# Macaron block, one core: a new order of the work ahead of the first exponential

## What is computed

```python
x = x + 0.5 * ffn(layernorm(x))          # layernorm inside ffn too; ternary weight, bias
x = x + attention(layernorm(x))          # q,k,v,o 512x512, rope, 64-token blocks, causal by block
x = x + 0.5 * ffn(layernorm(x))
# attention, per head (32 channels):
scores = einsum('bhqd,bhkd->bhqk', rope(q), rope(k)) * D**-0.5
ctx = einsum('bhqk,bhkd->bhqd', softmax(where(block_mask, scores, -inf)), v)
```

## Time and profile before

| | us |
|---|---|
| median of 3 runs (636.68 to 638.52) | 636.81 |
| the profiled execution | 636.18 |
| its span, from first to last instruction | 634.4 |
| TensorE busy (matmul) | 554.8 (87%) |
| VectorE busy | 409.6 (65%) |
| ScalarE busy | 310.5 (49%) |
| GpSimd busy | 238.9 (38%) |

### The profile page before, as it was taken

The page is one execution under the profiler, slowest core; times in us unless marked ns, Lnnn a source line. Parts: engine busy times, 40 slices in busy tenths (PEclk is TensorE's granted clock), DMA queues, the critical chain, the costliest instruction groups (busy, mean ns, idle before and its releaser), DMA issues.

```text
span 634.4 us, 10072 instructions
## 1 busy us (share of the span) xinstructions
PE 554.8 (87%) x3586; PEld 235.4 (37%) x3586; DVE 409.6 (65%) x782; ACT 310.5 (49%) x629; POOL 238.9 (38%) x200
## 2 busy tenths in 40 slices
PE   0785799679878999999999999999999898998866
PEld 0542545334323333333333333333344233343432
DVE  5999656626878668667677677677667822522462
ACT  0831622122215756756756666666656456661320
POOL 4001454443656547547556556556500100100100
PEclk9897899899979999999999999999999999999897
DMA  9930022363222125323123126323410021101011
GB/s 313 355 118 25 2 74 92 116 154 123 76 75 76 52 77 175 118 76 109 52 77 107 58 76 208 97 81 119 133 36 2 2 80 71 50 6 55 8 67 66
DMA packets 43602, 57.95 MB, mean 91 GB/s; under 512 B 3527, under 2 KB 34375, under 8 KB 42529
## 3 DMA queue, kind: packets, MB, share of 16 engines
q1 hardware_dynamic: 42972, 57.21, 27.5%
q10 hardware_dynamic: 580, 0.11, 0.1%
HBM read 32.01 MB, written 25.17 MB: 90 GB/s over the span
## 4 chain that ended last, share of the span: by engine, by line
PE 69%; DVE 23%; issue 3%; ACT 2%; DMA 1%; POOL 1%; SPq 0%; ACTq 0%; DVEq 0%; POOLq 0%
PE bank L956 11%; PE bank L1045 10%; PE bank L920 9%; PE bank L939 9%; PE bank L1055 8%; PE bank L874 7%; PE bank L884 6%; PE bank L993 5%; DVE rmax L815 5%; DVE stats L661 3%; DVE mparts L828 3%; DVE rmax L825 2%; PE bank L864 2%; DVE big L676 2%; DVE kst L676 1%
## 5 line engine op out<-in xcount | busy, mean ns | idle before, releaser
L815 DVE TENSOR_REDUCE rmax<-bank 128x1 f32<-128x512 f32 (+3 forms) x384 | 198.8, 551 | 107.7 <-PE bank L939 105.2
L609 ACT ACTIVATE big<-bank 128x512 f32<-128x512 f32 (+3 forms) x384 | 181.6, 492 | 141.9 <-PE bank L920 138.8
L939 PE MATMUL bank<-kst,qst 104*128 104x512 f16 (+3 forms) x384 | 126.2, 331 | 23.0 <-DVE rmax L815 16.4
L920 PE MATMUL bank<-qst,kst 106*128 106x512 f16 (+3 forms) x384 | 125.8, 329 | 3.1 <-ACT big L609 2.8
L502 POOL TENSOR_TENSOR rot<-t,sin_s 64x512 f32<-64x512 f32 x64 | 82.1, 1282 | 92.5 <-ACT t L602 89.8
L1045 PE MATMUL bank<-big,ones 128*32 128x512 f32 (+3 forms) x768 | 81.8, 498 | 0.0
L1055 PE MATMUL bank<-big,rows 128*32 128x512 f32 (+3 forms) x768 | 79.5, 486 | 0.0
L920 PEld LDWEIGHTS bank<-qst,kst 106*128 106x128 f16 x384 | 36.9, 96 | 89.9 <-issue 39.3
L511 POOL TENSOR_TENSOR rhl<-t,rhl 128x512 f16<-128x512 f32 x32 | 37.5, 1172 | 70.0 <-ACT rhl L623 70.0
L939 PEld LDWEIGHTS bank<-kst,qst 104*128 104x128 f16 x384 | 37.9, 99 | 64.2 <-DVE rmax L815 22.8
L956 PE MATMUL bank<-xh,wh 128*128 128x512 f16 x128 | 50.3, 393 | 6.3 <-DVE xl L697 5.9
(11 more groups left out here) (106 smaller groups left out, 688.6 us busy)
## 6 DMA issues: line engine op xcount, KB each, us to landing
spread<-rhl SPq DMA_DIRECT2D x32, 256.0 KB, 2.2
qst<-spread SPq DMA_DIRECT2D x16, 384.0 KB, 3.8
kst<-spread SPq DMA_DIRECT2D x16, 384.0 KB, 3.9
x<-rows SPq DMA_DIRECT2D x4, 1024.0 KB, 4.6
spread<-rhl SPq DMA_DIRECT2D x32, 128.0 KB, 2.1
rows<-in_L_attn_x_dram SPq DMA_DIRECT2D x3, 1024.0 KB, 15.4
xh<-ch SPq DMA_DIRECT2D x4, 512.0 KB, 5.5
xl<-cl SPq DMA_DIRECT2D x4, 512.0 KB, 6.7
```

Of the source, the lines that this page charges most:

```text
L609: nc.scalar.activation(probs[:, st % P_PLACES, h, 0:n], pb[u % 2][:, 0:n], ACT.Exp, scale=EXP_SCALE).then_inc(s_eb, 1)
L815: nc.vector.tensor_reduce(rmax[:, at:at + 1], a_bank(u)[:, 0:n], AX.X, ALU.max, negate=True).then_inc(s_max, 1)
L920: nc.tensor.matmul(pb[u % 2][:, 0:n], kst[0:ROWS_B, g % SETS, h, j * P:(j + 1) * P], qst[0:ROWS_B, g % SETS, h, q0:q0 + n], start=True, st ...
L939: nc.tensor.matmul(a_bank(u)[:, 0:n], qst[0:ROWS_A, g % SETS, h, i * P:(i + 1) * P], kst[0:ROWS_A, g % SETS, h, half * HALF:half * HALF + ...
```

## The change

The diff, cut where lines repeat what is told here. SECOND, the steps of the second batch and of its second block move, v_unit starts a tile every seven steps in the first batch and leaves steps 56 to 67 free; the second batch's transposes and products all use banks 3 and 4 in turn; loads and splits of weights come in the order q, v, k, o; waits are on high parts first and on low parts where they are read; the small operations of the maxima come after the reduction of the next step.

```diff
-        y1_bank = [bank[0:8], [bank[n % 5] for n in range(8)]]
+        y1_bank = [bank[0:8], bank[3:5] * 4]
         f1_bank = [bank[0:4] * 2, bank[3:5] * 4]
-        x_bank = [bank[4:8] + bank[0:4], [bank[n % 3] for n in range(8)]]
+        x_bank = [[bank[i] for i in (4, 0, 1, 2, 3, 4, 0, 1)], bank[3:5] * 4]
...
+        W_ORDER = (0, 2, 1, 3)
+        def weight_parts(i):
+            return W_ORDER.index(i) + 1
...
-            n, i = divmod(k - lag, 6)
-            if 0 <= n < BATCH * TILES:
-                return n // TILES, n % TILES, i
+            for n in range(BATCH * TILES):
+                i = k - lag - (7 * n if n < TILES else 68 + 6 * (n - TILES))
+                if 0 <= i < 6:
+                    return n // TILES, n % TILES, i
...
-        SECOND = 5
-        Y1_STEP = [7 + n for n in range(8)]
-        F1_STEP = [17 + 3 * r for r in range(8)]
-        S2_STEP = [30, 42]
-        N2_STEP = [34, 46]
-        X_STEP = [36 + n for n in range(4)] + [48 + n for n in range(4)]
+        SECOND = 18
+        N1_STEP = [24, 46]
+        Y1_STEP = [28, 30, 32, 34, 51, 53, 55, 57]
+        F1_STEP = [38, 41, 44, 47, 67, 70, 73, 76]
+        S2_STEP = [51, 80]
+        N2_STEP = [58, 85]
+        X_STEP = [61, 62, 63, 64, 88, 89, 90, 91]
...
@@ SyncE @@
             load_w(0, w_q)
+            load_w(2, w_v)
             load_w(1, w_k)
...
-            load_w(2, w_v)
...
-            sp.wait_ge(s_wl, 2)
-            mask_rows(0, 1)
             residual_out(0, 0)
             residual_out(0, 1)
+            sp.wait_ge(s_wl, weight_parts(1))
+            mask_rows(0, 1)
...
-                    if k == STEPS + 16 + 6 * bl:
+                    if k == X_STEP[4 * bl + 3] + 7:
                         columns_out(bl)
...
-                if k == STEPS + 10:
+                if k == X_STEP[3] + 4:
                     sp.wait_ge(s_wl, 4)
+                    sp.wait_ge(s_xtr[1], 4)
+                if k == X_STEP[7] + 4:
                     sp.wait_ge(s_xtr[1], 8)
                     mask_rows(1, SETS)
...
@@ GpSimd @@
-            rstd_of(1, 0, 5)
-            rstd_of(1, 1, 6)
-            roots = 6
+            roots = 4
...
+                    if k == N1_STEP[bl] - 2:
+                        rstd_of(1, bl, 5 + bl)
+                        roots = 5 + bl
...
@@ VectorE, ahead of the loop @@
-            for n in range(4):
-                weight_low(1, n)
+            ffn_update(4, f1_bank[0], blocks[0], s_ffn1[0], s_up1[0])
+            ffn_update(5, f1_bank[0], blocks[0], s_ffn1[0], s_up1[0])
             dve.wait_ge(s_ytr1[0], 4)
             normalize(0, 0, 3, blocks[0][0], y1[0][0], s_y2[0])
-            for r in range(4, 8):
-                ffn_update(r, f1_bank[0], blocks[0], s_ffn1[0], s_up1[0])
-            dve.wait_ge(s_up1[0], 8)
-            statistics(0, 1, 4, *ONCE, blocks[0][1])
+            ffn_update(6, f1_bank[0], blocks[0], s_ffn1[0], s_up1[0])
+            ffn_update(7, f1_bank[0], blocks[0], s_ffn1[0], s_up1[0])
             for n in range(4):
                 x_low(0, n)
             for n in range(4):
                 weight_low(2, n)
+            dve.wait_ge(s_up1[0], 8)
+            statistics(0, 1, 4, *ONCE, blocks[0][1])
+            for n in range(4):
+                weight_low(1, n)
...
@@ VectorE, in the loop @@
-                if k == 2:
-                    normalize(1, 0, 5, blocks[1][0], y1[1][0], s_y1[1])
-                    dve.wait_ge(s_x[1][1], 16)
-                    statistics(1, 1, 6, *TWICE, blocks[1][1])
...
+                if k == N1_STEP[0]:
+                    normalize(1, 0, 5, blocks[1][0], y1[1][0], s_y1[1])
+                if 36 <= k < 40:
+                    weight_low(3, k - 36)
+                if k == 40:
+                    dve.wait_ge(s_x[1][1], 16)
+                    statistics(1, 1, 6, *TWICE, blocks[1][1])
+                if k == N1_STEP[1]:
                     normalize(1, 1, 6, blocks[1][1], y1[1][1], s_y1[1])
-                if 16 <= k < 20:
-                    weight_low(3, k - 16)
...
-                if e := max_head(k, 0):
+                if e := max_head(k, 1):
...
@@ TensorE @@
+                    if u == 0:
+                        pe.wait_ge(s_xl[1], 8)
...
                         if g < 2:
                             pe.wait_ge(s_rows[g], 32)
-                            pe.wait_ge(s_xl[1], 8)
...
-                            pe.wait_ge(s_xl[0], 4 * (m // 2) + 4)
-                            pe.wait_ge(s_wl, 2)
+                            pe.wait_ge(s_xh[0], 4 * (m // 2) + 4)
...
+                    if g == 0 and CC in SLOTS[i]:
+                        pe.wait_ge(s_xl[0], 4 * (m // 2) + 4)
+                    if g == 0 and 2 * CC in SLOTS[i]:
+                        pe.wait_ge(s_wl, weight_parts(m % 2))
...
-                        pe.wait_ge(s_xl[b], 4 * (r // 4) + 4)
-                        pe.wait_ge(s_wl, 3)
+                        pe.wait_ge(s_xh[b], 4 * (r // 4) + 4)
...
+                    if i == 2:
+                        pe.wait_ge(s_xl[b], 4 * (r // 4) + 4)
+                    if i == 4:
+                        pe.wait_ge(s_wl, weight_parts(2))
...
                         pe.wait_ge(s_y1[1], 4 * (n // 4) + 4)
-                        pe.wait_ge(s_xl[0], 8)
-                        if n >= 5:
-                            pe.wait_ge(s_f1[1], n - 4)
+                        if n < 2:
+                            pe.wait_ge(s_xl[0], 8)
+                        elif n in (4, 5):
+                            pe.wait_ge(s_up1[1], n - 1)
+                        else:
+                            pe.wait_ge(s_f1[1], n - 1)
...
-                        if n >= 3:
-                            pe.wait_ge(s_xl[1], n - 2)
+                        if n < 2:
+                            pe.wait_ge(s_f1[1], n + 7)
+                        elif n in (4, 5):
+                            pe.wait_ge(s_up1[1], n + 3)
                         else:
-                            pe.wait_ge(s_f1[1], n + 6)
+                            pe.wait_ge(s_xl[1], n - 1)
...
-                        pe.wait_ge(s_f1[1], 5)
-                        if r >= 2:
+                        if r < 2:
+                            pe.wait_ge(s_f1[1], r + 3)
+                        elif r in (4, 5):
+                            pe.wait_ge(s_xl[1], r - 1)
+                        else:
                             pe.wait_ge(s_up1[1], r - 1)
```

More of the change, by code:

```diff
@@ L574, in _ @@
                 columns1(0, n)
[L575 to L578, removed]
+            for i in W_ORDER:
+                weight_high(i)
             for n in range(4):
@@ L724, in weight_low @@
             def weight_low(i, cc):
-                dve.wait_ge(s_wh, i + 1)
+                dve.wait_ge(s_wh, weight_parts(i))
                 last = nc.vector.scalar_tensor_tensor(wl[:, i, cc, :], stage[i][:, cc, :], W_SCALE, wh[:, i, cc, :],
@@ L903, in _ @@
             for cc in range(CC):
+                if cc:
+                    pe.wait_ge(s_up1[0], 4 + cc)
                 transposed(x_bank[0][cc], y1[0][0], cc, s_xtr[0])
```

## The result

The changed kernel takes 612.93 us (median of 4, 610.56 to 614.11) against 637.66 in the same comparison; the ratio is 0.9606 with a 95% interval of 0.9569 to 0.9642. Twice more, in other comparisons, it was 0.9631 (0.9613 to 0.9649) and 0.9651 (0.9631 to 0.9671). The profiled execution took 612.61, its span 610.8.

A forecast was written before the change was run, and what follows sets the result against it. TensorE was taken to bound the exponential stretch (372.9 of 389.0 us busy), while the two stretches before lost 37 us. Span 634.4 - 21 - 4.6 = 608.8, 610.5 us after adjustment and rounding; range 602 to 624, the forecast's own 604 to 617.

The forecast's parts named there:

- Part 1: Start of the step loop: step 0 waits for high parts only and comes at 45.0 us, 5.8 us earlier.
- Part 2: Steps 0 to 58: 46.7 us of TensorE work plus 7.6 of waits, so step 59 is reached at 99.3 us.
- Part 3: Steps 59 to 117: 55.1 us of work plus waits at three places; step 118 at 169 us, 21 us earlier.
- Place (a): Steps 61 to 64, waiting for a normalization and the fourth projection's way: idle some 7 us, then 2 us for half clock.
- Place (b): Steps 80 to 91: VectorE has 16.4 us of work against TensorE's 11.4, costing 5 us.
- Place (c): Last transposes before step 118 each wait for a fresh low part, 1 us; first value product behind them, 0.5.
- Part 4: Maxima's small operations one step later: about 0.3 us saved at each of 16 fourth-score waits, 4.6 us; bounds 0 and 13.
- slow clock through the stretch: Rival: frequent waits keep the granted clock at 1.2 GHz from step 60 on; time 653 us, chance 0.03.
- gain paid back in the exponentials: Rival: something starting no earlier (GpSimd, transfers) sets the exponential stretch and takes the gain back; 636 us, chance 0.02.
- Half the gain: Rival: VectorE's long operations hold the score banks more often, two more wait and half-clock pairs; 623 us, or 618; chance 0.17.

The follow-up runs named there:

- e7: The changed kernel unchanged, run again as the measure for three others: 615.17 us, ratio 0.9651 to the kernel before.
- e5: The changed kernel with step 0 waiting also for the low parts and the value weights' low part: 617.70 us, ratio 0.9696.
- e10: Changed kernel, copy before scale and shift, rotary of four tiles held behind normalizations, one normalization before the weight split, two tiles' high parts two steps later: 610.09 us.
- e4: The changed kernel with one GpSimd wait: rotary of step 81's tile starts only after the second batch's last normalization: 610.11 us, ratio 0.9581.
- e1: The changed kernel with the small operations of the maxima back in their old place: 617.37 us, ratio 0.9680.
- e8: The kernel before with only the small operations of the maxima one step later: 629.19 us, ratio 0.9869.
- e9: The changed kernel with ScalarE's projection copy ahead of the scale and shift, and two tiles' rotary held behind normalizations: 610.54 us, ratio 0.9577.
- e11: The changed kernel with the small operations in their old place for the first group's four heads only: 612.00 us, ratio 0.9594.

## Why the prediction was right

610.5 us were forecast, 612.9 measured; 26.3 us of gain, 24.7 measured. The total is nearer than its terms, and that is luck: the start of the loop came 3.0 us late and steps 59 to 117 took 3.1 more, while the exponential stretch gave 2.3 more than its term and the tail behind it 1.6 that no term had (0.2 in e7). Two slips in the prediction's sum are small: 16 x 0.3 is 4.8 and not 4.6, and 611.2 was rounded to 610.5. The steps, by their own numbers:

- **Part 1, start of the loop**: 45.0 forecast, 47.97 measured, 45.2 in e7. The chain was right to 0.2 us; the rest is the granted clock of the products ahead, which the earlier trace rows show at full rate, so the forecast took it as given. In nine traces of kernels that start the products alike the distance from the first product to step 0 was 18.3 us where all products ran at full clock (e7), 19.7 to 20.1 in seven whose first products took 1.91 us, and 21.2 in the changed kernel's first profile, where this lasted longest. e5 shows that a later start costs time at the end.
- **Part 2, steps 0 to 58**: 54.3 forecast, 54.2 measured. The work was counted; the waits came to the same sum from other places. Step 18 waited 2.98 (forecast 2.1), its normalization took 4.74 (nearly 5). Step 28 did not wait (2.7 forecast). A copy and a feed-forward product took 0.87 and 0.97 us. The idle times come to 5.1 us where 7.6 were forecast, and a half clock 3.4 us long behind step 18, which the forecast left out, cost 1.7. That the sum met to 0.1 us is in part luck. The sentence that this would be 5 us less if the normalizations took 1.91 is not borne out: only one of the two waits was there to be gained, and in e10, where all normalizations took 1.9, holding the rotary back brought waits of its own and the stretch took 54.6.
- **Part 3, steps 59 to 117**: 69.7 forecast, 72.8 and 73.5 measured. Place (a): idle 4.9 us instead of 7, half clock 5.5 us long instead of 4; its wait is ScalarE's queue at step 60 and the normalization, not the transfer. Place (b): 1.42, 0.57, 3.10 and 0.24 make 5.3 us (5 forecast). What was left out is the half clock behind it, 4.7 us at 0.64, which e4 removes along with the wait. Place (c): 0.3 instead of 1.5; 0.8 at step 111 was not foreseen. In all TensorE was idle 11.3 us (13.5 forecast), and the granted clock of 0.93 over 72.8 us cost up to 5.1 (2 forecast). So the term that was too small is the clock's, in (b) above all; e7 has 10.7 us of idle time and up to 6.8 of clock.
- **Part 4, small operations**: 4.6 forecast. The exponential stretch shows 6.5 to 7.6 (e1), 5.8 (e8). Per group of four heads it is 46.86 us in e1 and 45.73 in the changed kernel, for two waits: 0.5 to 0.6 each and not 0.3. The mechanism (fourth score at once, fifth waits) is as described, 0.34 and 0.17 us at the fifth instead of 0.86 and 0.64 at the fourth. In the medians only 2.3 to 3.1 us of it are seen (e1). The forecast took the small operations' 1.86 us as their own length. It is mostly GpSimd's, as e4 shows for one head: they took 1.9 to 2.3 us in the 27 heads of the kernel before with rotary work beside them, and 0.57 in the four heads behind with none (timeline of VectorE, the last of the three operations, beside the rotary and alone):

```profile
250.45 1.11 DVE L828 SCALAR_TENSOR_TENSOR mparts<-rmax,mparts 128x8 f16<-128x8 f32 x1
...
461.91 0.17 DVE L828 SCALAR_TENSOR_TENSOR mparts<-rmax,mparts 128x8 f16<-128x8 f32 x1
```

  No run keeps the rotary off them all along the exponential stretch; whether that would do more than the later place is open.
- **Rivals**: no slow clock through the stretch (0.93 of full over steps 59 to 117), no gain paid back in the exponentials. Half the gain: one such pair of long operation and half clock did appear, at steps 80 to 91, at 5.3 us of waiting and 1.7 of clock (3.4 in e7), near the 4 and 2.6 that the rival had priced it at; there was one and not two more.

The Trainium skill (SBUF — State Buffer, "Who interferes with whom") says that VectorE in its two-port modes, which a tensor_scalar can enter, contends with GpSimd for a shared pair of ports: whoever issues first has the pair for the whole instruction, and the other waits. The runs agree: four normalizations took 1.91 us alone and 5.84 where rotary work ran all along (e5), with 2.86, 3.66 and 4.74 in between, and e4 brought one from 3.66 to 1.91 by moving GpSimd alone. In e5 it was VectorE that paid: GpSimd's operations took 1.33 us each beside it, and 1.27 in e4 with no normalization beside them.

## What to carry to other kernels

Count the work of a stretch in instructions and subtract: where the busiest engine has 62.7 us to do in 82.6, a better order can have part of the difference. Here the waits came in other places than foreseen and the sum still met, which one case does not make a rule. A wait of 3 us on TensorE costs more than itself when the clock falls behind it; look at the window behind every wait. Ask for every vector instruction that is moved, and for the small ones too, what GpSimd does at its new place: removing such an overlap pays where the wait ends a chain (e4, 5 us for one wait) and not where the held-back work is itself next in line (e9, e10). And when a stretch of two profiles differs by 2 us, look at the clock in it before giving the edit the credit (e1, e11).

## What the runs showed of the hardware

The granted clock changes from one execution to the next with the same instructions before it. In the products ahead of the loop of the changed kernel it was 1.2 GHz until 32.7 us in one profile and full throughout in another (e7, from 26.9), worth 2.7 us of the loop's start. Behind the waits of steps 80 to 91 it was 1.00 in e1 and 0.66 in e11, with the same instructions and waits ahead of it, worth 2.7 us from step 88 to 93. A single profile's clock in such a place is not to be taken as given for the next kernel.

A window's clock of 1.00 can also mean that the trace holds no clock record there. In e4 the record begins at 30.59 us, and the windows before it are given as 1.00, although the four matmuls at 27.76 took 1.91 us, the duration of 1.2 GHz:

```profile
27.76 1.91 PE L891 MATMUL bank<-wt,xh 128*128 128x512 f16 x4
```

```profile
27.00:33.00 6.00, 5.62 (x19) 2.23 (x20) 3.42 (x6) 6.00 (x7) 0.00 (x0) 1.00 0.57 214
```

In e9, whose record begins earlier, the clock stands at 0.50 from 27.0 to 29.5 and the four matmuls took 1.91 us as well. The durations are the check.

A small operation of VectorE can lose more in proportion beside GpSimd than a large one: 0.17 us became 1.11 (128x8), where four of 128x512 went from 1.91 to 5.84.

Two edits worth 20 and 8 to 10 us alone were worth 22 to 25 together. The traces show the waits that the second removes in both kernels; why the medians do not add is not settled.
